# Bias loads, weight order and query transposes in the opening of an attention and FFN kernel

## The reference

```python
xn = _layernorm(x, axis=-1)
q = (xn @ Wq.T + bq).reshape(B, S, 32, 32)
k = (xn @ Wk.T + bk).reshape(B, S, 32, 32)
v = (xn @ Wv.T + bv).reshape(B, S, 32, 32)
scores = jnp.einsum('bshd,bsgd->bshg', q, k) * inv_sqrt_d
scores = jnp.where(scores > THRESH, scores, -jnp.inf)
attn = jax.nn.softmax(scores, axis=-1)
out = jnp.einsum('bshg,bsgd->bshd', attn, v).reshape(B, S, Hd)
attention = out @ Wo.T + bo
...
ffn = (silu(xn @ Wg.T) * (xn @ Wu.T)) @ Wd.T
return x + attention + ffn
```

## Time and profile before

| | |
|---|---|
| median of 3 runs | 2087.65 us (2086.99 to 2087.65) |
| the profiled execution's own time | 2088.32 us |
| its span | 2086.5 us |
| PE busy | 2023.0 us, 97% of the span |
| DVE busy | 1595.7 us, 76% |
| ACT busy | 1260.0 us, 60% |
| POOL busy | 1347.1 us, 65% |
| mean granted TensorE clock | 0.992 |

### The profile page before, as it was taken

The page is one execution under the profiler, slowest core; times in us unless marked ns, Lnnn a source line. Parts: engine busy times, 40 slices in busy tenths (PEclk is TensorE's granted clock), DMA queues, the critical chain, the costliest instruction groups (busy, mean ns, idle before and its releaser), DMA issues. The chain is left out here.

```text
span 2086.5 us, 36966 instructions
## 1 busy us (share of the span) xinstructions
PE 2023.0 (97%) x10892; PEld 979.4 (47%) x10892; DVE 1595.7 (76%) x1584; ACT 1260.0 (60%) x2020; POOL 1347.1 (65%) x769
## 2 busy tenths in 40 slices
PE   9999999999998899899999999999999999999986
PEld 6555555555554444334444444444444444444434
DVE  6576776676665300599999999999999999999996
ACT  5578778778776311245666666666666666566652
POOL 1445554554643000058888888889888988898885
PEclk9999999999999999999999999999999999999998
DMA  9463453553554353221213121221122212211226
GB/s 268 91 131 86 106 133 83 109 132 84 110 117 132 101 173 117 51 71 46 50 47 81 48 50 45 74 57 50 45 66 64 50 45 63 67 46 50 60 82 251
DMA packets 329581, 184.41 MB, mean 88 GB/s; under 512 B 269124, under 2 KB 305988, under 8 KB 329543
## 3 DMA queue, kind: packets, MB, share of 16 engines
q1 hardware_dynamic: 329542, 183.90, 34.0%
HBM read 94.73 MB, written 25.17 MB: 57 GB/s over the span
## 5 line engine op out<-in xcount | busy, mean ns | idle before, releaser
L1250 POOL TENSOR_TENSOR acc<-acc,lower 128x1024 f32<-128x1024 f32 x327 | 770.9, 2369 | 161.6 <-ACT lower L961 161.4
L664 PE MATMUL banks<-xt,lower 128*128 128x512 f16 x3584 | 857.2, 379 | 13.5 <-DVE lower L1140 8.7
L961 ACT ACTIVATE lower<-banks,down_scale 128x512 f32<-128x512 f32 x654 | 413.6, 683 | 381.9 <-PE banks L689 293.2
L1140 DVE SCALAR_TENSOR_TENSOR lower<-banks,gate_scale,lower 128x1024 f32<-128x1024 f32 x392 | 478.9, 1277 | 143.6 <-PE banks L664 143.5
L664 PEld LDWEIGHTS banks<-xt,lower 128*128 128x128 f16 x3584 | 343.4, 98 | 458.3 <-DVE lower L1140 74.2
L510 PE MATMUL banks<-wt,xt_tile 128*128 128x512 f16 x2304 | 537.9, 380 | 0.0
L1140 DVE SCALAR_TENSOR_TENSOR lower<-banks,up_scale,lower 128x1024 f32<-128x1024 f32 x392 | 479.1, 1277 | 26.7 <-PE banks L664 23.6
L689 PE MATMUL banks<-lower 128*128 (+1 forms) x1792 | 461.9, 381 | 12.1 <-DVE acc L1193 11.9
L1212 POOL TENSOR_TENSOR stacks<-unit,stacks 128x512 f16<-128x512 f32 x192 | 245.4, 1302 | 311.3 <-ACT stacks L788 311.1
L510 PEld LDWEIGHTS banks<-wt,xt_tile 128*128 (+1 forms) x2304 | 215.9, 98 | 215.8 <-issue 1.1
L689 PEld LDWEIGHTS banks<-lower 128*128 (+1 forms) x1792 | 172.2, 98 | 230.5 <-DVE acc L1193 12.9
(11 more groups left out here) (64 smaller groups left out, 1329.4 us busy)
## 6 DMA issues: line engine op xcount, KB each, us to landing
lower<-in_L_ffn_gate_q_dram SPq DMA_DIRECT2D x28, 512.0 KB, 3.7
lower<-in_L_ffn_up_q_dram SPq DMA_DIRECT2D x28, 512.0 KB, 4.4
lower<-in_L_ffn_down_q_dram SPq DMA_DIRECT2D x28, 512.0 KB, 3.9
x_tile<-in_L_attn_x_dram SPq DMA_DIRECT2D x16, 512.0 KB, 3.6
xt_scratch<-xt_tile SPq DMA_DIRECT2D x16, 512.0 KB, 2.8
ctx_scratch<-ctx_parts SPq DMA_DIRECT2D x64, 128.0 KB, 2.1
lower<-ctx_scratch SPq DMA_DIRECT2D x4, 2048.0 KB, 8.4
xt<-xt_scratch SPq DMA_DIRECT2D x4, 2048.0 KB, 15.9
```

Of the source, the lines that this page charges most:

```text
L664: last = mm(psum[:, 2 * (slot % 3) + c, :], gu_t[:, mat, g, :], xt[:, (2 * half + c) * CT:(2 * half + c + 1) * CT, part, g, :], start=(par ...
L961: run(down_tmp[:, buffer, c * BANK:(c + 1) * BANK], psum[:, 6 + c, :], ACT.Copy, scale=scale)\
L1140: v.scalar_tensor_tensor(out=acc_of[:, half, :], in0=gu_pair(slot % 3), scalar=scale[:, :, :].rearrange("p t k -> p (t k)")[:, bass.ds(t * ...
L1250: g.tensor_tensor(acc[:, half, ho, :], acc[:, half, ho, :], down_tmp[:, buffer, :], ALU.add).then_inc(down_added, 1)
```

## The change

The bias spread on PE and ACT is taken out, and with it `ones`. Instead SP loads each bias straight into 128 partitions, with one source row read 128 times: bq behind block 10, bk behind block 13, bv behind block 15. DVE waits for bq's and bk's landing ahead of the first unit copy that uses them. bv lands in `s_c` in the order (head, dimension), and POOL copies it to (dimension, head) after its second unit.

A block of Wv is loaded in one piece like the others. The order (dimension, head) is made on leaving PSUM: ACT's HI part is one instruction with a permuted output, and DVE's LO part is four instructions, one for each head of the block.

Blocks 22 and 23 are transposed one after the other, without a quarter between them; ten quarters are left then. The quarters from 16 on, which make V, wait until all 24 blocks are made. The four Q batches of tile 0 stand behind quarters 17, 19, 21 and 23, and so do their copies on ACT and DVE.

```diff
...
-        ones = sb(whole, "ones", [1, P], F32)
...
-        bias_spread = sem("bias_spread")
-        bias_ready = sem("bias_ready")
+        bias_turned = sem("bias_turned")
...
+        LAST_W = 3 * KT - 2
+        BATCH_AT = {17: 0, 19: 1, 21: 2, 23: 3}
+        BIAS_AT = {10: 0, 13: 1, 15: 2}
         def opening(weights, first_x, quarter, second_x):
...
             for w in range(ROWS, 3 * KT):
-                quarter(w - ROWS)
+                if w < LAST_W:
+                    quarter(w - ROWS)
-            for s in range(3 * KT - ROWS, 3 * KT):
+            for s in range(LAST_W - ROWS, 3 * KT):
         def steps_of(i, s):
...
-        bias_rows = (s_c[0:1, :, :].rearrange("p g d -> p (g d)"), p_c[0:1, :, :].rearrange("p g d -> p (g d)"),
-                     p_stack[0:1, :, :, :].rearrange("p g n h -> p (g n h)").bitcast(F32)[:, 0:H])
-        def bias_pair(n):
-            return psum[:, (0, 2, 6)[n]:(0, 2, 6)[n] + 2, :].rearrange("p b c -> p (b c)")
+        bias_rows = s_c[:].rearrange("p g d -> p (g d)")
         def rows_landed(w):
-            return sum(16 if n < 2 * KT else 16 * TG for n in range(w % ROWS, w + 1, ROWS))
+            return 16 * (w // ROWS + 1)
         def weight_pair(w):
+        def weight_source(w):
+            return weight_pair(w).rearrange("p (k h d) -> p k h d", h=TG, d=DH)
+        def weight_place(w, part):
+            place = wt[:, w // KT, part, :, :]
+            at = slice((w % KT) * TG, (w % KT + 1) * TG)
+            if w // KT == V:
+                return place.rearrange("p k (d h) -> p k h d", h=NH)[:, :, at, :]
+            return place.rearrange("p k (h d) -> p k h d", d=DH)[:, :, at, :]
         def batch_bank(m):
...
         def _(pe):
-            pe.wait_ge(const_ready, 3)
+            pe.wait_ge(const_ready, 2)
             def weights(w):
                 pe.wait_ge(w_loaded[w % ROWS], rows_landed(w))
-                if w in (1, 2):
-                    pe.wait_ge(bias_ready, 3)
...
             def first_quarter(s):
-                pe.wait_ge(w_hi, 4 * (s // 4) + 4)
-                pe.wait_ge(w_lo, 4 * (s // 4) + 4)
+                made = 4 * (s // 4) + 4 if s < 16 else 3 * KT
+                pe.wait_ge(w_hi, made)
+                pe.wait_ge(w_lo, made)
                 project(0, s)
+                if s in BATCH_AT:
+                    batch(0, BATCH_AT[s])
             def turn_wo(n2):
...
-            def spread_bias(n):
-                pe.wait_ge(bias_loaded[n], 16)
-                for c in range(2):
-                    last = mm(bias_pair(n)[:, c * BANK:(c + 1) * BANK], ones[:], bias_rows[n][:, c * BANK:(c + 1) * BANK],
-                              start=True, stop=True)
-                last.then_inc(bias_spread, 1)
             def first_tile():
-                for n in (Q, K, V):
-                    spread_bias(n)
                 opening(weights, lambda: None, first_quarter, lambda w: None)
-                for m in range(4):
-                    batch(0, m)
...
             def weights(w):
-                run(wt[:, w // KT, HI, :, (w % KT) * P:(w % KT + 1) * P],
-                    weight_pair(w).rearrange("p (k r) -> p k r", r=P), ACT.Copy,
-                    scale=W_SCALE).then_inc(w_hi, 1)
+                run(weight_place(w, HI), weight_source(w), ACT.Copy, scale=W_SCALE).then_inc(w_hi, 1)
             def root(i):
...
+                if BATCH_AT.get(s, 1) % 2 == 0:
+                    batch_copy(0, BATCH_AT[s])
...
-            def bias_out(n):
-                act.wait_ge(bias_spread, n + 1)
-                src = bias_pair(n)
-                if n == V:
-                    dst = bias_qkv[:, V, :].rearrange("p (d h) -> p d h", h=NH)
-                    src = src.rearrange("p (h d) -> p d h", d=DH)
-                else:
-                    dst = bias_qkv[:, n, :]
-                run(dst, src, ACT.Copy).then_inc(bias_ready, 1)
             def first_tile():
-                for n in (Q, K, V):
-                    bias_out(n)
                 opening(weights, lambda: x_part(0), first_quarter, second_x)
-                batch_copy(0, 0)
-                batch_copy(0, 2)
...
             def weights(w):
-                at = slice((w % KT) * P, (w % KT + 1) * P)
-                v.scalar_tensor_tensor(out=wt[:, w // KT, LO, :, at],
-                                       in0=weight_pair(w).rearrange("p (k r) -> p k r", r=P), scalar=W_SCALE,
-                                       in1=wt[:, w // KT, HI, :, at], op0=ALU.mult,
-                                       op1=ALU.subtract).then_inc(w_lo, 1)
+                for at in ([slice(0, TG)] if w // KT != V else [slice(n, n + 1) for n in range(TG)]):
+                    last = v.scalar_tensor_tensor(out=weight_place(w, LO)[:, :, at, :],
+                                                  in0=weight_source(w)[:, :, at, :], scalar=W_SCALE,
+                                                  in1=weight_place(w, HI)[:, :, at, :], op0=ALU.mult,
+                                                  op1=ALU.subtract)
+                last.then_inc(w_lo, 1)
             def unit_copy(i, u):
...
             def first_quarter(s):
-                if s == 4:
-                    dve.wait_ge(bias_ready, 3)
+                if s in (4, 12):
+                    dve.wait_ge(bias_loaded[s // 8], 16)
+                if s == 20:
+                    dve.wait_ge(bias_turned, 1)
+                if BATCH_AT.get(s, 0) % 2:
+                    batch_copy(0, BATCH_AT[s])
             def second_x(w):
...
             def first_tile():
                 opening(weights, lambda: x_part(0), first_quarter, second_x)
-                batch_copy(0, 1)
-                batch_copy(0, 3)
...
         def _(pool):
-            g.memset(ones[:], 1.0).then_inc(const_ready, 1)
...
             def first_units():
                 for u in range(6):
+                    if u == 1:
+                        pool.wait_ge(bias_loaded[V], 16)
+                        g.tensor_copy(bias_qkv[:, V, :].rearrange("p (d h) -> p d h", h=NH),
+                                      bias_rows.rearrange("p (h d) -> p d h", d=DH)).then_inc(bias_turned, 1)
...
-                if w < 2 * KT:
-                    sp.dma_start(w_rows[:, w % ROWS, :], (Wq, Wk)[w // KT][(w % KT) * P:(w % KT + 1) * P, :])\
-                        .then_inc(w_loaded[w % ROWS], 16)
-                else:
-                    by_dim = Wv.rearrange("(h d) k -> d h k", d=DH)
-                    for n in range(TG):
-                        sp.dma_start(w_rows[n * NH:(n + 1) * NH, w % ROWS, :], by_dim[(w % KT) * TG + n, :, :])\
-                            .then_inc(w_loaded[w % ROWS], 16)
+                sp.dma_start(w_rows[:, w % ROWS, :], (Wq, Wk, Wv)[w // KT][(w % KT) * P:(w % KT + 1) * P, :])\
+                    .then_inc(w_loaded[w % ROWS], 16)
             def load_x(i):
...
-            for n, b in enumerate((bq, bk, bv)):
-                sp.dma_start(bias_rows[n], b.rearrange("(a n) -> a n", a=1)).then_inc(bias_loaded[n], 16)
             for w in range(ROWS):
                 load_w(w)
             for w in range(ROWS, 3 * KT):
                 load_w(w)
+                if w in BIAS_AT:
+                    n = BIAS_AT[w]
+                    sp.dma_start((bias_qkv[:, Q, :], bias_qkv[:, K, :], bias_rows)[n],
+                                 (bq, bk, bv)[n].rearrange("(a n) -> a n", a=1).broadcast_to((P, H)))\
+                        .then_inc(bias_loaded[n], 16)
```

## The result

The changed kernel takes 2124.63 us (median of 5 runs) against 2087.65 us: ratio 1.0174, 95% interval 1.016 to 1.0188. It is 37 us slower where I forecast 1 us faster, and far outside my range. Its profiled execution took 2125.0 us.

The account below looks back on a forecast made before the run. PE bounds the kernel (97% busy), so the opening's shift passes to the end: -5.4 + 1.7 + 4.3 + 1.7 - 3.4 = -1.1 us on the median 2087.65, giving 2086.6 us; range 2082.0 to 2091.5.

Parts of the forecast that it names:

- the chain: V's blocks: LO part, unit copy, ACT's unit parts, then next HI part; DVE sets the pace, LO 23 ending at 64.9.
- The mark: PE's start of token tile 1's second quarter, 78.35 us before; its shift, forecast -1.1 us, passes to the end one for one.
- lead at block 8: Opening: block 8 lands at 20.5 instead of 25.9, 5.4 us sooner, between 3.4 and 8.3.
- clock behind the gap at block 8: After PE stands 3.7 us ahead of block 8, the half-level clock costs 1.7 us, between 0 and 3.4.
- V's blocks up to quarter 16: Quarter 16 waits for LO 23 and begins at 64.9 instead of 60.6; PE stands 4.3 us ahead of it.
- quarter 16 to the mark, with its clock: From quarter 16 on: batches among quarters gain 3.4 us, the half-level clock behind the wait costs 1.7.
- Edit 3: V's parts: four LO pieces take 1.70 us, 0.48 more for each of eight blocks; ACT's permuted write stays at 1.02.
- Rival B: V's pieces on DVE are dear: 0.60 us each instead of 0.42, sum +4.5, 2092.2 us, slower; chance 0.14.
- Edit 1: Opening: biases leave the queue heads; x's transpose is issued at 9.7, 8.2 us sooner, and block 8 lands at 20.5.
- Edit 2: Bias loads among blocks 11 to 15: they delay landings by 1.3 to 2.6 us, cost 0 under 3 us of cover.
- Edit 4: Blocks 22 and 23 together, V's quarters after all blocks: PE stands 4.3 us ahead of quarter 16.
- Edit 5: Q batches among quarters, from quarter 16 on: 14.3 us where it was 17.7, a gain of 3.4 us.

Follow-up runs that it names:

- The probe: Kernel before, each of the eight V blocks written in another pattern, only instruction durations counting: on ACT 4.72 us at 16-byte steps, 1.02 with a permuted read.
- the run with ACT mended: The changed kernel, but ACT writes V's HI parts in runs of four heads, DVE's four pieces unchanged: 2112.48 us, ratio 1.0113.
- the biases alone: Kernel before with only the biases loaded by broadcast behind blocks 10, 13 and 15: 2086.53 us, ratio 0.9988.
- edit 3 alone: Kernel before with only Wv in whole rows, permuted writes by ACT and DVE, and quarter 16's wait for all 24 blocks: 2129.7 us, 1.0192.

## Why the prediction was wrong

The path and the chain were right, and one term, the price of V's parts, was not. The mark's shift, by the prediction's own steps:

| step | predicted | measured |
|---|---|---|
| lead at block 8 | -5.4 | -4.3 (21.54 against 25.88) |
| clock behind the gap at block 8 | +1.7 | +2.1 (block 9 at 25.86 against 28.10) |
| V's blocks up to quarter 16 | +4.3 | +38.9 (97.33 against 60.63, and the lead of 2.2) |
| quarter 16 to the mark, with its clock | +1.7 - 3.4 = -1.7 | -1.6 (16.17 against 17.72) |
| sum | -1.1 | +35.1 |

**Edit 3 is the step that failed**, in two sentences of it. "ACT's permuted write stays at 1.02: the copy of bv wrote such an order, 128 bytes apart, in 1.02" is false, and could have been seen in the code. In `bias_out` both sides are named in the order (dimension, head): the destination is then dense, and it is the read from PSUM that is permuted. The probe has that case too, and it takes the same 1.02. So the kernel before had no row of a 2-byte write apart on either engine, and I took an unknown for a known. And "four pieces take 1.70 us", from L1066, rests on runs of eight values; the pieces took 4.7. Four dense pieces took 1.42 in the probe, so the count of pieces was not the trouble.

The chain itself held. With 4.7 in place of 1.70 for DVE alone and the lead of 2.2 it gives quarter 16 at 86.7 and the mark at 101.0, or 102.7 with the low clock; the run with ACT mended has 84.69 and 101.11. The 12.4 us more of the change are ACT's 4.7 in the same chain. DVE's pieces in the change:

```profile
57.99 18.69 DVE L1002 SCALAR_TENSOR_TENSOR wt<-banks,wt 128x256 f16<-128x256 f32 x16 [5.79 <-ACT wt L760]
...
82.97 14.26 DVE L1002 SCALAR_TENSOR_TENSOR wt<-banks,wt 128x256 f16<-128x256 f32 x12 [5.77 <-ACT wt L760]
```

and with ACT mended, where the same two waits are 2.13 us:

```profile
70.79 13.79 DVE L1005 SCALAR_TENSOR_TENSOR wt<-banks,wt 128x256 f16<-128x256 f32 x12 [2.13 <-ACT wt L763]
```

Ahead of block 16's pieces DVE stands 3.61 us in the change and not at all there. These three waits differ by 10.9 us together. Of the rest, 0.9 us is the opening, where block 9 starts at 25.86 in the change and at 24.99 with ACT mended, and 0.7 us is the pieces themselves, which are a little slower in the change.

**Rival B** named the mechanism for DVE, with 0.60 a piece; it was 1.18, and on ACT as well. I had bounded it by nearly half as much again as the nearest row, for no reason. Its chance of 0.14 leaned on the false row of bv. The Trainium skill ("SBUF — State Buffer", section "Door 1: The DMA port swizzle") had said that accesses which go to a new line of 16 bytes pay a penalty. The probes agree on the 16 bytes for writes, and show that the price depends on the width of what is written: 4.6 ns for single 2-byte values, 1.8 to 2.0 ns for 4-byte words. I had set it aside on the strength of that misread row.

**Edit 1** was right in kind: the transpose was issued at 9.48 into a full queue and held SP for 6.42 us, to 15.9, where I had it free at 14.6. So block 8 came at 21.54 in place of 20.5, behind a gap of 4.40, at half level. That half level cost 2.1 us up to block 9 here and in the biases alone, and 1.4 in three other executions with this opening, so 1.7 was right in size, and its nearness to any one run is luck. One reading was wrong beside it: rows 4's transposes of 421 ns in the kernel before were put down to a low clock, but the granted clock was 1.00 there. Behind the gap at block 8 of the change the granted clock is 0.50 and the transposes take the same 421 ns. **Edit 2** cost nothing, as said: in the change no block from 9 to 15 waits for its landing. With blocks 8 and 9 loaded first, block 11 waited 1.79 us, and this wait was gone when the bias loads went further back. POOL's copy of bv took 1.96 us in its wait. **Edit 4** costs 0.83 us of idle PE ahead of quarter 16 once the writes are not slow. **Edit 5** was right at the mark (3.2 of the 3.4 us, alone), but part of its gain is the clock, and that differs from one execution to another.

## What to carry to other kernels

Before a row is taken as the price of an access pattern, read from the code on which side the permutation lies: the same shape took 1.02 us with a permuted read and 4.7 with a permuted 2-byte write. Where an order must change, let it change on the read from PSUM or in PE's output, and keep at least a 4-byte word together in what ACT and DVE write. A cost that no row shows should be bounded by an experiment or by a factor of several, above all where it stands in a loop that two engines share.

## What the runs showed of the hardware that I had not expected

- A 2-byte write alone in its 16 bytes costs ACT and DVE alike about 4.6 ns (4.72 and 4.69 us for 1024 values); a 4-byte one 1.8 to 2.0 ns; two or more float16 values side by side cost no more than dense ones at the engine's pace (1.04 and 1.00 on ACT).
- PE wrote its transposes into PSUM 16 bytes apart at the same 272 ns as densely.
- The same idle time of 1.98 us of PE was followed by the half level in the kernel before (0.50 in 76 to 78 us), and not with the biases alone (1.00 in 70 to 75) or with edit 3 alone (1.00 in 110 to 118).
- The float32 transposes took 421 ns both at a granted clock of 0.50 (block 8 of the change) and at one of 1.00 (14.5 to 19.7 us of the kernel before), and 272 ns later at 1.00. So the granted clock alone does not tell which of the two durations a stretch has.
